# A fifth shared batch with banks of its own ahead of the routed tiles, the output projection of two batches inside attention, and pad rows written by two queues

## The reference

```
x = x + attention(layernorm(x))            # 16 heads of 16, relative position bias, output projection Wo
t = layernorm(x)                           # 4096 rows
shared = gelu(t @ sw1 + sb1) @ sw2 + sb2   # the expert that every row goes through
logits = t @ gate_w.T + expert_bias        # 7 routed experts
w = softmax(top2(logits))                  # each row goes to two of them
x = x + shared + sum over its two experts of w * (gelu(t @ rw1 + rb1) @ rw2 + rb2)
```

## Time and profile before

| | us |
|---|---|
| median of 3 runs (839.57 to 842.66) | 841.91 |
| the profiled execution | 837.18 |
| its span, first to last instruction | 835.4 |
| PE busy, share of the span | 777.1, 93% |
| DVE busy | 619.8, 74% |
| ACT busy | 478.5, 57% |
| POOL busy | 254.1, 30% |

### The profile page before, as it was taken

One profiled execution on the slowest core, in us unless ns is written; L12 is line 12 of the kernel. 1 busy time (PEld: TensorE's weight loads), 2 busy tenths in 40 slices (PEclk: granted clock), 3 DMA queues, 4 the chain that ended last, 5 costly groups with the idle time before them and its releaser, 6 DMA issues. The chain is left out here.

```text
span 835.4 us, 18227 instructions
## 1 busy us (share of the span) xinstructions
PE 777.1 (93%) x6217; PEld 540.0 (65%) x6217; DVE 619.8 (74%) x1928; ACT 478.5 (57%) x720; POOL 254.1 (30%) x407
## 2 busy tenths in 40 slices
PE   5899889999999999999998999788897899999997
PEld 2777646665666666666565565564554489999964
DVE  5666489888888888889886880577665557777855
ACT  2444306667666667666665676274554168778730
POOL 1122111211111121121111110257677426555640
PEclk9999959999999999999998999998998999999999
DMA  4999884633464344553353553545432545556758
GB/s 120 272 351 363 277 235 120 165 101 103 135 151 142 104 126 122 146 146 102 100 162 121 175 194 125 147 159 180 164 125 83 153 140 145 170 149 217 221 208 322
DMA packets 74631, 140.75 MB, mean 168 GB/s; under 512 B 14520, under 2 KB 34640, under 8 KB 74366
## 3 DMA queue, kind: packets, MB, share of 16 engines
q1 hardware_dynamic: 62962, 116.91, 46.1%
q0 software_dynamic: 9792, 19.54, 7.1%
q10 hardware_dynamic: 1788, 3.18, 1.1%
HBM read 85.71 MB, written 56.78 MB: 171 GB/s over the span
## 5 line engine op out<-in xcount | busy, mean ns | idle before, releaser
L740 DVE CUSTOM_DVE_ANT_0 sums<-pS,near 128x512 bf16<-128x512 f32 x512 | 329.3, 688 | 49.6 <-PE pS L806 41.3
L773 ACT ACTIVATE prob<-pE 128x1024 f32<-128x1024 f32 x256 | 248.4, 1022 | 150.3 <-PE pE L831 150.2
L831 PEld LDWEIGHTS pE<-bandT,place 64*128 64x128 f32 x2048 | 166.4, 189 | 12.6
L831 PE MATMUL pE<-bandT,place 64*128 64x244 f32 (+2 forms) x2048 | 163.2, 271 | 0.0
L806 PE MATMUL pS<-k_st,q_st 48*128 48x512 f32 x512 | 138.6, 477 | 6.4 <-DMA k_st<-k_parts 3.8
L806 PEld LDWEIGHTS pS<-k_st,q_st 48*128 48x128 f32 x512 | 62.7, 192 | 116.2 <-DVE nmax L740 88.9
L845 PE MATMUL pC<-prob,v_aug 128*32 128x512 f32 x1024 | 136.6, 608 | 1.0 <-ACT ctx_sb L781 1.0
L823 PE MATMUL pE<-q_st,k_st 62*128 62x512 f32 x512 | 114.9, 406 | 2.3 <-issue 2.3
L1124 POOL DMA_INDIRECT expert_rows<-rb,xr x76 | 76.9, 1012 | 67.0 <-DVE rb L1337 48.7
L1108 POOL DMA_INDIRECT routed_rows<-xr,slot_i x64 | 66.6, 1041 | 31.7 <-issue 19.5
L1646 PE MATMUL pD<-w2p,hT 128*128 x456 | 63.8, 289 | 0.6 <-DVE hT L1330 0.6
(11 more groups left out here) (193 smaller groups left out, 1059.9 us busy)
## 6 DMA issues: line engine op xcount, KB each, us to landing
xr<-routed_rows SPq DMA_DIRECT2D x38, 258.0 KB
q_st<-q_parts SPq DMA_DIRECT2D x64, 128.0 KB, 2.7
k_st<-k_parts SPq DMA_DIRECT2D x64, 128.0 KB, 2.9
ctx<-ctx_sb SPq DMA_DIRECT2D x32, 256.0 KB, 2.8
q_parts<-qk SPq DMA_DIRECT2D x14, 512.0 KB, 7.9
k_parts<-qk SPq DMA_DIRECT2D x14, 512.0 KB, 7.4
near<-bias_by_distance SPq DMA_DIRECT2D x16, 448.0 KB, 5.2
xr<-expert_rows SPq DMA_DIRECT2D x14, 512.0 KB, 6.4
```

The costliest lines, as they stand in the source:

```text
L740: dve.tensor_tensor_reduce(sums[:, r % 4], pS[:, unit % PS], near[:, hg % 2, j, lead:lead + S], -1.0, BIG, ALU.add, ALU.min, nmax[:, j, t: ...
L773: act.activation(prob[:, par, 2 * step:2 * step + 2], pE[:, 2 * (step % 2):2 * (step % 2) + 2], ACT.Exp).then_inc(exp_done, 1)
L831: ins = pe.matmul(pE[:, bank + side, a:z], place[rows, half], bandT[rows, (quad // 2) % 2, pair, part, lead:lead + z - a], start=False, st ...
```

## The change

It has four parts.

1. Batches 0 and 1 are projected inside `attend`. PE does `project_out(0)` behind step 5 of the last unit and `project_out(1)` behind its last step, both into banks of pS that the scores no longer need. DVE adds the residuals of both there, POOL inverts both deviations, ACT normalises batch 0 and PE turns it; batch 2's context is loaded and multiplied there too. The deviation buffers `rstd` and `nbias` are doubled. SP writes the inverted denominators one unit earlier (u == 2 for u == 3). In `finish`, the loop begins with the gate of batch 0. The reciprocal of the second half of the denominators stands behind `choose(0)`.
2. Context loads are issued one turn earlier, and the x rows of batch 4 are loaded in turn 1, since their place is lent to batch 0.
3. Batch 4 of the shared expert (`IN_GAP`) has the banks pX[:,1] and pX[:,0,1] and hidden rows in `cn` of its own, and the up half of batch 5 (`TILES_FROM`) is done ahead of the tiles. Its down half stays behind them.
4. Of the 7 writes of pad rows, SP issues 4 and ACT 3.

```diff
@@ attend, SP
-                        if b < BE:
+                        if b < BE - 2:
                             sp.dma_start(g["x1c"][:, b - 2], g["x_p"][b]).then_inc(g["x_late"], 16)
...
-                    if u == 3:
+                    if u == 2:
                         wait_apart(sp, passed, den_inv, 1)
                         sp.dma_start(den_rows(rden_dram, S, DW, 0), den[:]).then_inc(rden_out, 16)
...
+                    wait_apart(sp, passed, g["early"]["wo_mm"], 2 * k + 2)
+                    load_context(sp, g, 2 + k)
                     wait_apart(sp, passed, evac, n + 1)
@@ attend, DVE
                 for b in range(2):
                     context(dve, g, b)
+                for b in range(2):
+                    dve.wait_ge(g["x_ld"][b], 16)
+                    add_residual(dve, g, pS[:], g["x1"][:, b], b)
+                context(dve, g, 2)
@@ attend, ACT
                 copy_ctx(NI - 2)
+                act.wait_ge(g["early"]["rstd2d"], 1)
+                for t in range(TT):
+                    act.activation(first_rows_of(g)[:, t], g["x1"][:, 0, t], ACT.Identity, ...)
                 copy_ctx(NI - 1)
+                for c in range(MC):
+                    act.wait_ge(g["early"]["xT2_mm"], c + 1)
+                    act.activation(first_turned(g)[:, c], pE[:, c], ACT.Copy).then_inc(g["early"]["xT2"], 1)
@@ finish, SP
+                for b in range(BE - 1, B):
+                    sp.dma_start(x1v(b), g["x_p"][b]).then_inc(x_late, 16)
...
-                    if i >= 1 and i + 3 < B:
-                        sp.wait_ge(s["wo_mm"], 2 * (i + 1) + 2)
-                        load_context(sp, g, i + 3)
+                    if i + 4 < B:
+                        sp.wait_ge(s["wo_mm"], 2 * (i + 2) + 2)
+                        load_context(sp, g, i + 4)
+                    if i == 1:
+                        sp.wait_ge(s["u_mm"], 2)
+                        sp.dma_start(x1v(BE - 2), g["x_p"][BE - 2]).then_inc(g["x4_ld"], 16)
...
-                for e in range(NR):
+                for e in range(PADS_BY_SP):
@@ finish, DVE
-                residual(0)
-                residual(1)
-                dve.wait_ge(s["den_ld"], 16)
-                dve.reciprocal(den[:], den[:]).then_inc(s["den_inv"], 1)
...
                     choose(i)
+                    if i == 0:
+                        dve.wait_ge(s["den_ld"], 16)
+                        dve.reciprocal(den[:], den[:]).then_inc(s["den_inv"], 1)
...
                 for b in range(B):
                     second_rows(b)
-                for b in range(TILES_FROM, B):
-                    add(b)
+                    if b == 1:
+                        add(TILES_FROM)
+                    elif b == OWN - 1:
+                        add(OWN)
+                add(B - 1)
@@ finish, ACT
-                for b in range(EARLY + 1, TILES_FROM):
-                    hidden(b, 0)
-                    hidden(b, 1)
-                    shares(b)
+                hidden(IN_GAP, 0)
+                shares(IN_GAP)
+                hidden(IN_GAP, 1)
+                act.wait_ge(s["pads_done"], 1)
+                for e in range(PADS_BY_SP, NR):
+                    row = act.value_load(pad_at[0:1, e:e + 1], min_val=0, max_val=NR * RS)
+                    act.dma_start(xs_dram[bass.ds(row, TS), :], g["pad_rows"][e]).then_inc(pad_out[0], 16)
+                hidden(TILES_FROM, 0)
+                hidden(TILES_FROM, 1)
```

More of the change, by code:

```diff
@@ L51 @@
 CB = 5
+IN_GAP = 4
 TILES_FROM = 5
@@ L71 @@
 ADD_FROM = NFIRST + 3
+PADS_BY_SP = 4
 def band_start(kh):
@@ L159, in layer_kernel @@
         ctx_sb = sb("ctx_sb", [P, 2, S], F32)
+        stats = sb("stats2", [P, TT, 6], F32)
+        mv = sb("mv2", [P, TT, 2], F32)
+        half = sb("half2", [P, TT], F32)
+        rtmp = sb("rtmp2", [P, 2, TT], F32)
+        rstd = sb("rstd2", [P, 2, TT], F32)
+        nbias = sb("nbias", [P, 2, TT], F32)
+        xn_first, x4_ld = sem("xn_first"), sem("x4_ld")
+        early = {n: sem(n) for n in "wo_mm x1_add st2 var2 chain2 rstd2d xT2_mm xT2".split()}
         cn_ld, rden_out = [sem("cn_ld0"), sem("cn_ld1")], [sem("rden_out0"), sem("rden_out1")]
@@ L570, in context, with first_rows_of, first_turned, project_out @@
     dve.tensor_tensor(cn[:, b % 2], cn[:, b % 2], rb[:, b % 2], ALU.mult).then_inc(g["c_ready"], 1)
+def first_rows_of(g):
+    return g["x1c"][:, BE - 3]
+def first_turned(g):
+    return g["x1c"][:, BE - 4].rearrange("p t d -> p (t d)").rearrange("p (c s) -> p c s", c=MC)
+def project_out(pe, g, bank, b):
+    s, cn, wo_f = g["early"], g["cn"], g["wo_f"]
+    pe.wait_ge(g["c_ready"], b + 1)
+    for t2 in range(2):
+        if b >= 1:
+            pe.wait_ge(s["x1_add"], 2 * b - 1 + t2)
+        for u in range(2):
+            t = 2 * t2 + u
+            for c in range(MC):
+                ins = pe.matmul(bank[:, t2, D * u:D * u + D], cn[:, b % 2, c, t:S:TT], wo_f[:, c],
+                                start=c == 0, stop=c == MC - 1)
+        ins.then_inc(s["wo_mm"], 1)
+def add_residual(dve, g, bank, xb, b):
+    s, stats, mv = g["early"], g["stats"], g["mv"]
+    for t2 in range(2):
+        dve.wait_ge(s["wo_mm"], 2 * b + t2 + 1)
+        dve.tensor_tensor(xb[:, 2 * t2:2 * t2 + 2], bank[:, t2].rearrange("p (u d) -> p u d", u=2),
+                          xb[:, 2 * t2:2 * t2 + 2], ALU.add).then_inc(s["x1_add"], 1)
+    dve.wait_ge(s["x1_add"], 2 * b + 2)
+    if b >= 1:
+        dve.wait_ge(s["rstd2d"], b)
+    for t in range(TT):
+        dve.bn_stats(stats[:, t], xb[:, t]).then_inc(s["st2"], 1)
+    for t in range(TT):
+        dve.wait_ge(s["st2"], 4 * b + t + 1)
+        dve.bn_aggr(mv[:, t], stats[:, t]).then_inc(s["var2"], 1)
+def invert_deviation(pool, g, b):
+    s, mv, rstd, nbias = g["early"], g["mv"], g["rstd"][:, b % 2], g["nbias"][:, b % 2]
+    pool.wait_ge(s["var2"], 4 * b + 4)
+    _, ins = rsqrt_steps(pool, g["passed"], mv, g["half"][:], rstd, g["rtmp"], s["chain2"], 7 * b)
+    ins.then_inc(s["chain2"], 1)
+    pool.wait_ge(s["chain2"], 7 * b + 6)
+    pool.tensor_tensor(nbias, mv[:, :, 0], rstd, ALU.mult).then_inc(s["chain2"], 1)
+    pool.wait_ge(s["chain2"], 7 * b + 7)
+    pool.tensor_scalar(nbias, nbias, -1.0, None, ALU.mult).then_inc(s["rstd2d"], 1)
 def keep_turning(pe, g, bank, count):
@@ L694, in _ @@
                 pool.sem_clear(g["retired"])
+                pool.memset(g["half"][:], -0.5).then_inc(half_made, 1)
                 for par in range(2):
@@ L789, in _ @@
                 copy_ctx(NI - 2)
+                act.wait_ge(g["early"]["rstd2d"], 1)
+                for t in range(TT):
+                    act.activation(first_rows_of(g)[:, t], g["x1"][:, 0, t], ACT.Identity, bias=g["nbias"][:, 0, t:t + 1],
+                                   scale=g["rstd"][:, 0, t:t + 1]).then_inc(g["xn_first"], 1)
                 copy_ctx(NI - 1)
+                for c in range(MC):
+                    act.wait_ge(g["early"]["xT2_mm"], c + 1)
+                    act.activation(first_turned(g)[:, c], pE[:, c], ACT.Copy).then_inc(g["early"]["xT2"], 1)
             @block.tensor
@@ L859, in slot @@
                             values(n - 1, (u + 1) % 2, step // 2, first and u == 1)
+                        if n == NI - 1 and step == 5:
+                            pe.wait_ge(g["small_ld"], 16 * SMALL)
+                            pe.wait_ge(max_done, MAX0 + 16 * NI)
+                            project_out(pe, g, pS[:], 0)
                 for step in range(STEPS + LEAD):
@@ L865, in _ @@
                         slot(4 * quad + u, u, quad, first=quad == 0, last=quad == QUADS - 1)
+                project_out(pe, g, pS[:], 1)
                 for t in range(TT):
                     values(NI - 1, 1, t)
-                pe.wait_ge(g["small_ld"], 16 * SMALL)
-                pe.wait_ge(max_done, MAX0 + 16 * NI)
-                keep_turning(pe, g, pS[:, 0, 0:D], 5)
+                pe.wait_ge(g["xn_first"], TT)
+                for c in range(MC):
+                    for t in range(TT):
+                        ins = pe.transpose(pE[:, c, P * t:P * t + P], first_rows_of(g)[:, t, P * c:P * c + P], g["ident"][:])
+                    ins.then_inc(g["early"]["xT2_mm"], 1)
+                keep_turning(pe, g, pS[:, 2, 0:D], 6)
 def finish(nc, mk, g):
@@ L991, in finish @@
                  "xt_mm xhi xlo wc_hi wc_lo up_mm hhi hlo dn_mm ev_done yf_acc y_acc").split()
-        s = {n: sem(n) for n in names}
+        s = {**g["early"], **{n: sem(n) for n in names}}
         scat = [sem(f"scat{r}") for r in range(XR)]
@@ L1518, in _ @@
                         gelu(k + 2, experts[k + 2])
-                for b in range(TILES_FROM, B):
+                shares(TILES_FROM)
+                shares(OWN)
+                for b in (OWN, B - 1):
                     hidden(b, 0)
                     hidden(b, 1)
-                    if b == OWN:
-                        shares(OWN - 1)
-                        shares(OWN)
                 shares(B - 1)
```

191 lines of the change are left out of this document (85 added, 106 removed).

## The result

The changed kernel took 829.67 us in the median of four executions (827.48 to 831.64), the kernel before 841.76 (four, 839.57 to 842.66): ratio 0.9841, 95% interval 0.9801 to 0.988. I had forecast 834.1, faster by 0.9%. The direction is right, and the time is at the lower edge of my range (829.5); by the ratio, 0.9841 of 841.91 or 828.5, it lies just beyond it. The gain is half as large again as the 7.8 us that I had added up. The mean of the four ratios is 0.9885, some 9.7 us. Both the size of my terms and the size of the first result are therefore in question. Medians are over all executions, while a ratio leaves out those that took over 1.5% longer than the fastest of their kernel, six in the table of the experiments.

A forecast was written before the change was run, and what follows sets the result against it. PE was taken to bound the stretch before the loop, POOL's scatters the loop. Front 6.6, gap 1.1 and tail 0.1 sum to 7.8 us, so 841.91 becomes 834.1, 0.9% less; range 829.5 to 839.5.

The forecast's parts named there:

- The front arrives: End of attention to first scatter: early projections bring logits 8.3 us earlier, less 1.7 for the reciprocal; 6.6 us gained.
- The gap: Between scatter loop and tiles: PE's reordered work ends at 671.7 for 672.76, pads out of its way; 1.1 us gained.
- The tail: Behind the last tile: PE's work ends 1.9 us earlier, less 1.8 for a clock fall; 0.1 us gained.
- PE now idles for 2.9 us there: Behind the last tile: PE waits for DVE's last evictions, ending at 804.3, before transposing batch 5's shares.
- I expect a fall here too: Behind the last tile: granted clock falls to half after the idle, costing 1.75 or 3.3 us; the shorter was taken.
- The 1.9 us of the term: Behind the last tile: PE's listed work reaches 824.8 where the last down half before began at 826.7.
- bound of +3.5: Behind the last tile: the gain if evictions, held 1.80 us by something called remote, come at once.
- The tail keeps its clock: Rival, behind the last tile: idle too short for a fall; gain 9.5 us, 832.4, or 830 with early evictions; chance 0.22.
- The loop gives some back: Rival, scatter loop: clock falls again and POOL waits for slot numbers, costing 3.3 us, 837.5; chance 0.20.
- the front does not arrive: Rival, end of attention: late context 0, POOL's second chain or batch 2's context eats the gain; 838 to 844; chance 0.13.
- slower: Rival, last attention unit: a late context 0 holds up PE's projection and all behind it, above the old time; chance 0.05.

The follow-up runs named there:

- pads_only: Kernel before with only the pad writes split, four on SP and three on ACT: 830.5 us for 831.05, ratio 1.0013.
- chain_late: Changed kernel with POOL's second chain (deviation of batch 1) behind the change of block: 833.54 us, ratio 0.9872 to the kernel before.
- two_late_short: Changed kernel with POOL's second chain and the second reciprocal late, and a filler of 4 instructions, not 12: 823.88 us, ratio 0.9857 to the kernel before.
- pads_sp: Changed kernel with all seven pad writes on SP: 836.91 us, ratio 0.9887 to the kernel before.
- after_third: Changed kernel run again as it is, beside the kernel before: 827.3 us for 836.3, ratio 0.9884.
- adds_last: Changed kernel with DVE's adds of batches 5, 6 and 7 again behind all second-choice rows: 833.76 us, ratio 0.9890 to the kernel before.
- recip_late: Changed kernel with the reciprocal of the second denominators behind the slot numbers of batch 0: 831.48 us, ratio 0.9848 to the kernel before.
- after_again: Changed kernel run again as it is, beside the kernel before: 823.12 us for 831.05, ratio 0.9921.

## Why the prediction was right in its direction and short in its size

The profiles give each stage without the spread of attention. Means over the profiles of the changed kernel (four) and of all kernels that have the stage as before (five):

| stage | before | changed | gain | forecast |
|---|---|---|---|---|
| end of step 5 of the last unit to the first scatter | 36.9 | 30.5 | 6.3 | 6.6 |
| first scatter to the end of the last | 109.8 | 110.2 | -0.4 | 0 |
| end of the last scatter to the first up half | 12.4 | 11.2 | 1.2 | 1.1 |
| end of the last tile to the end | 35.3 | 31.5 | 3.8 | 0.1 |

The sum is 10.9; the four comparisons gave 7.0 to 12.1 us in the medians. One of the five in the third row is pads_only, which has part 4 there; without it the row has 12.6 and a gain of 1.4.

- *The front arrives, 6.6 us forecast.* Right: denominators at 499.55, projections of 4.1 us without a wait ahead of the first, the gate at full clock, the reciprocal's 1.75 us on the path. Two errors cancelled in part. Batch 1's chain on POOL, put at 530.2, ended at 531.5, and the change of block took 1.5 to 2.1 us, not 0.55 (chain_late shows POOL's arrival as the cause, worth 1.2 us). Against that, three of the four other profiles with the old front took 1.2 to 1.5 us more than the one I had read.
- *The gap, 1.1 us.* Right in size, though not by its parts. PE bound the gap, as forecast, and the pads (four at 1.67 us on SP) were out of its way; a piece at half clock (up half 3.02 us for 1.9) ate part in the first profile, not in the three later ones.
- *The tail, 0.1 us.* This is the step that failed, a term mis-sized by 3.3 to 3.7 us: the idle behind the last tile was put 1.8 us too long, and a fall of the clock of 1.8 us was charged that did not come. "PE now idles for 2.9 us there" was built on evictions that end at 804.3, held by a stall called remote for 1.80 us; in seven of twelve profiles the idle is 1.13. Why the evictions come later in the others stays open. "I expect a fall here too" came true in one of the four profiles of the changed kernel; where it came, it cost about 1.7 us (two_late_short, pads_sp) or 2.9 (after_third), which is what I had priced (1.75 or 3.3). The 1.9 us of the term also counted on the new order of DVE's adds without naming it: with the old one PE waits, and 2.1 of the 3.8 us on PE are gone (adds_last). And I took the old tail at its 33.8, though with its wait for the add of batch 5 it falls in two of five profiles and takes 37 to 38. I had put down a bound of +3.5; I should have weighed the fall by its frequency on both sides, instead of charging it whole to the new one.
- *The rivals.* "The tail keeps its clock" (0.22) is what happened, with the early evictions that it put at 830. "The loop gives some back" happened in part: over all 15 profiles with the new front the loop took 110.9 us for 109.8, the longest 114.1 and 114.9. Of "the front does not arrive" one condition came true, the block's end that POOL's second chain sets, but it cost 1.2 us and not all of the gain; "slower" did not happen. Context 0 was there at 511.68 + 1.23 = 512.9, half a microsecond ahead of PE.
- *The first result itself* lies 3 us beyond the mean of the four comparisons (12.1 for 9.0 in the medians). With a spread of 3 to 4 us between executions, a mean of four against four is uncertain by over 2, so nothing more need be behind it.

What stays open: the front is worth 6 us at the first scatter, 5.9 if the loop's 0.4 is taken off, but 3.4 to 4.7 us where it was measured on top of gap and tail, and 0.4 and 3.5 alone. Falls of the clock later in the loop and in the old tail may account for some of it. The profiles, one to four for each kernel, do not show the rest, and the intervals are as wide as the difference.

## What to carry to other kernels

An expected fall of the clock is a chance, not a cost: weigh it on both sides of the comparison, by how often each place shows it in several profiles. Where a block ends, look at who arrives last, since the hand-over took 0.45 us when PE came last and 1.5 to 2.1 when POOL was as late; an operation that nobody needs ahead of the hand-over belongs behind it. An add that frees a bank for PE should not stand behind additions that wait for DMAs: moving it up took away a wait of 0.6 to 2.4 us (six profiles with the old order), and with it a place where the clock fell in two of them.

## What the runs showed of the hardware

- One and the same kernel spread from 823.6 to 836 us on one chip, with three of 35 executions up to 840.9, and its mean granted clock, 0.979 down to 0.961, went with it (correlation -0.88).
- Behind an idle of the same length (2.17 us) the granted clock was 0.50 in one kernel's profile (two_late_short) and 1.00 in another's (recip_late). The falls near the last tile stood behind idles of 2.09 to 5.66 us; one in the old tail stood behind 1.04 and 0.88 us (pads_only).
- Chips differed in the loop of tiles: 125.8 us on two of them, with no stall called remote, 130 to 136 on another, with stalls of up to 3.3 us in which ACT and DVE stood though nothing in the trace held them.
- An issue of a pad row took 1.1 us on ACT's queue in every profile, and on SP's from 1.15 us (4.58 / 4, after_again) to 2.3 (9.09 / 4, adds_last).
